# Mamba step sizes in later states, and the 64 sequences cut 11, 14, 14, 14, 11

## The chip, the cores and the metric

The kernel runs on one core of a Trainium2 chip. The core has five engines that run their own instruction queues in order and wait for one another on semaphores: TensorE (PE; its weight loads are PEld), VectorE (DVE), ScalarE (ACT), GpSimd (POOL) and SyncE (SP), which issues most transfers. The metric is device time in microseconds of a whole execution.

## The reference

The program is one audio tower of several layers; the change touches the first attention layer only. There a three-layer Mamba and a two-way LSTM run on the same input, and their outputs are fused. There are 64 sequences of S = 33 time steps. The part that is timed here is the Mamba step-size dt and the state scan:

```python
xdbl = jnp.einsum('blc,ec->ble', u, xpw)
dt = jax.nn.softplus(jnp.einsum('blr,cr->blc', dt_in, dw) + db)
A = -jnp.exp(Alog)
def step(h, inp):
    dt_t, B_t, C_t, u_t = inp
    dA = jnp.exp(dt_t[..., None] * A)
    h = dA * h + (dt_t * u_t)[..., None] * B_t[:, None, :]
    y = jnp.einsum('bcn,bn->bc', h, C_t)
...
y = ys.transpose(1, 0, 2) + u * Dp
y = y * _silu(z)
```

u is a causal convolution of the input's first projection (four taps), z the second half of the projection. There are 256 channels (two halves of 128, called h) and 16 states for each channel.

## The kernel before

The Mamba stage is `mamba_lstm`. The 64 sequences are cut into five **chunks** (`SEQS`, line 414), and each chunk of each of the three layers is an **item** j = 0 to 14; `item(j)` (line 430) gives layer, first column and number of columns n (sequences x 33). Within an item the loop runs over the 16 **states** k = 0 to 15; g = 16 j + k counts all 240. Channels lie on the partitions, and the two channel halves lie side by side, so that an operation over both is "double-width" (858 columns for 13 sequences).

One state takes one step of a four-engine pipeline:
- ScalarE, `decay(g)`, line 894: dA = exp(dt * A), two operations into a PSUM pair; it may run two states ahead of the scan (dA has two buffers).
- GpSimd, line 1126: dBu = du * B, also two states ahead.
- VectorE, `scan(g)`, line 1053, the recurrence over all sequences of the chunk (h restarts because dA is 0 at each first step), then `weigh(g - 1)`, line 1063: times C.
- TensorE, `add(g - 1)`: two matmuls with the identity (each runs as two passes) that sum the states in PSUM bank pair py.

SyncE loads B and C for two states at a time, four buffers deep.

Beside the states run, at fixed k, the preparation of later items and the end of earlier ones. All engines' order is written out by hand: in its loop over g each engine does its state work first and then whatever its own table of k says. What matters here, for item j:
- TensorE: the deltas (input of softplus) of item j+1 at k = 0 and 1; the convolution of item j+2 at k = 3 and 5 (`project`, one channel half each, eight passes), z at 7 and 8; LSTM matmuls at 2, 6 and 14.
- ScalarE: softplus of item j+1, in a form that is exact for large and small values and takes a chain of operations on `mag`, `e` and `low`: `delta` at k = 3, 4, 5 and `steps` at 7 and 8. u of item j+2 is copied out of PSUM at k = 7 and 8 (line 781), each copy waiting for one half of the convolution. Four small LSTM gate operations stand at k = 2, 6 and 10 (`lstm_gates`, lines 871 and 872, the last writes cz), the cell's tanh at 3, 7, 11 (line 876). Two table loads stand at k = 7 and 9 in the items with LSTM, two around the silu at k = 11.
- VectorE: the LSTM cell `lstm_c` at k = 1, 5 and 9 (line 1025 first; it needs the gates that ScalarE makes at k = 2, 6 and 10), `lstm_h` behind it at 2, 6, 10; the gate product yz of item j-1 at k = 1; at k = 8 `soften(j + 1)` (three double-width operations, lines 995, 998, 1003: dt, then du = dt * u) and `back(j - 2)` (line 1017, layer norm's scaling into m).
- GpSimd at k = 10 waits for du of item j+1 and for m.

The LSTM has 33 time steps, three to an item, and so fills items 0 to 10. In front of the loop everything for item 0 is prepared in one go (the head), and behind it the last item goes through output projection, layer norm and fusion (the tail).

Of the kernel before, what the change touches and what calls it, by code (L numbers as in the profile page):

```python
# [15 lines left out]
S = 33  # L16
# [393 lines left out]
    _at += _width  # L410
MWID = _at

SQ = 13
SEQS = [13, 13, 13, 13, 12]
NSC = len(SEQS)
SCW = SQ * S
NI = NL * NSC
LAST = NI - NSC
BG, NBS = 2, 4
# [10 lines left out]
def item(j):  # L430

    l, c = j // NSC, j % NSC
    return l, c * SCW, SEQS[c] * S


def by_seq(ap):
# [4 lines left out]
def mamba_lstm(nc, cst, w_dram, cw_dram, lstm_dram, xn, m, hT, norm):  # L441

    with ExitStack() as ctx:
# [313 lines left out]
        def _(act):  # L757
# [45 lines left out]
            def delta(j, k):  # L803
                l, at, n = item(j)
                if k == 3 or k == 4:
                    h = k - 3
                    act.wait_ge(d_ready, 2 * j + h + 1)
                    if j >= 1:
                        act.wait_ge(dt_done, j)
                    a(mag[:, h, 0:n], bank(j, f"d{h}")[:, 0:n], ACT.Abs).then_inc(mag_ready, 1)  # L810
                    a(pos[:, h, 0:n], bank(j, f"d{h}")[:, 0:n], ACT.Relu).then_inc(d_read, 1)
                if k == 4:
                    act.wait_ge(mag_ready, 2 * j + 2)
                    a(e[:, :, 0:n], mag[:, :, 0:n], ACT.Exp, scale=-1.0).then_inc(e_ready, 1)
                if k == 5:
                    a(low[:, :, 0:n], mag[:, :, 0:n], ACT.Relu, scale=-1.0, bias=edge[:, 4:5]).then_inc(capped, 1)
                    act.wait_ge(capped, j + 1)
                    a(low[:, :, 0:n], low[:, :, 0:n], ACT.Exp, scale=-1.0, bias=edge[:, 4:5]).then_inc(w_ready, 1)
                    act.wait_ge(w_ready, j + 1)
                    a(low[:, :, 0:n], low[:, :, 0:n], ACT.Square, scale=KAPPA, bias=edge[:, 1:2]).then_inc(sq_w_ready, 1)  # L820

            def steps(j, k):
                l, at, n = item(j)
                if k == 7:
                    act.wait_ge(sq_w_ready, j + 1)
                    a(low[:, :, 0:n], low[:, :, 0:n], ACT.Ln, bias=edge[:, 2:3]).then_inc(low_logged, 1)
                    act.wait_ge(e_ready, j + 1)
                    a(e[:, :, 0:n], e[:, :, 0:n], ACT.Ln, bias=edge[:, 0:1]).then_inc(ln_ready, 1)
                if k == 8:
                    act.wait_ge(low_logged, j + 1)  # L830
                    a(low[:, :, 0:n], low[:, :, 0:n], ACT.Exp, scale=-0.5, bias=edge[:, 3:4]).then_inc(low_ready, 1)

# [75 lines left out]
            project(0, 14)  # L908
            for k in (3, 4, 5):
                delta(0, k)  # L910
            for k in (7, 8):
                steps(0, k)
            act.wait_ge(l_loaded, 112)
            a(whh[:, :, :, :], whh[:, :, :, :], ACT.Copy, scale=0.5).then_inc(lw_ready, 1)
# [17 lines left out]
            for g in range(NI * DST):  # L932
# [18 lines left out]
                    project(j + 2, k)  # L951
                if k == 7 and j < LSTM_ITEMS:
                    nc.scalar.preload_act_table_set("natural_log_exp_and_others")
                if k in (7, 8) and j + 1 < NI:
                    steps(j + 1, k)
                if k == 7 and j >= 2:
                    logs(j - 2)
                if k == 9 and j < LSTM_ITEMS:
                    nc.scalar.preload_act_table_set("exp_and_others")
                if j == NI - 1 and k == 10:  # L960
# [22 lines left out]
        def _(dve):  # L983
# [83 lines left out]
            for g in range(NI * DST):  # L1067
                j, k = g // DST, g % DST
                scan(g)
                if g >= 1:  # L1070
                    weigh(g - 1)
                if j < LSTM_ITEMS:
                    if k in (1 if j else 2, 5, 9):
                        lstm_c(PER_ITEM * j + (k - 1) // 4)
                    if k in (2 if j else 3, 6, 10):
                        lstm_h(PER_ITEM * j + (k - 2) // 4)
                if j >= 1 and k == 1:
                    gate(j - 1)
                if k == 8:
                    if j + 1 < NI:  # L1080
                        soften(j + 1)
                    if j >= 2:
                        back(j - 2)
                if k == 15 and j >= LAST + 2:
                    fuse(j - LAST - 2)
            weigh(NI * DST - 1)
# [7 lines left out]
        def _(pool):  # L1094
# [16 lines left out]
            for g in range(NI * DST):  # L1111
                j, k = g // DST, g % DST
                l, at, n = item(j)
                q = g // BG
                if k == 0:
                    pool.wait_ge(du_done, j + 1)
                if k == 10:
                    if j + 1 < NI:
                        pool.wait_ge(du_done, j + 2)
                    if j >= 2:  # L1120
                        pool.wait_ge(m_scaled, j - 1)
                if g % BG == 0:
                    pool.wait_ge(b_loaded[q % NBS], 16 * (q // NBS + 1))
                if g >= 2:
                    pool.wait_ge(h_ready, g - 1)
                g_.tensor_tensor(dBu[:, g % 2, 0:2 * n].rearrange("p (a n) -> p a n", a=2), du[:, j % 2, :, 0:n],  # L1126
                                 Bs[:, q % NBS, k % BG, 0:n].unsqueeze(1).broadcast_to([128, 2, n]), ALU.mult).then_inc(dBu_ready, 1)
                if j in (1, NSC + 1) and k in (2, 4, 6, 8):
                    build(l + 1, k // 2 - 1)
# [2765 lines left out]
```

## Time and profile before

| | us |
|---|---|
| runs (3): median | 2210.42 |
| lowest and highest | 2202.44, 2212.16 |
| the profiled execution | 2202.75 |
| its span | 2200.9 |
| TensorE busy | 1873.3 (85%) |
| VectorE busy | 1626.5 (74%) |
| ScalarE busy | 1327.4 (60%) |
| GpSimd busy | 1013.3 (46%) |

The span is the time between first and last instruction. Shares are over the whole program; the Mamba stage is only its first 840 us or so, after which other layers with other limits follow. An engine's row in the timeline gives the start, the duration, what it does, and in brackets how long the engine sat idle before it and which operation of which engine ended that.

### The profile page before, as it was taken

How to read it: one execution, taken by the hardware profiler on the slowest of the kernel's cores; microseconds unless marked ns; L12 is line 12 of the kernel's file. 1: busy time of each engine (PE TensorE's matmuls, PEld its weight loads, DVE VectorE, ACT ScalarE, POOL GpSimd, SP SyncE). 2: the span in 40 equal slices, each digit the busy share in tenths (PEclk: the TensorE clock that was granted, in tenths of full speed). 3: DMA queues.
4: the chain of work that ended last, by engine and by line, in shares of the span. 5: the costliest groups of instructions: out<-in, count | busy, mean ns of one | idle time of the engine just before them, and what ended most of it. 6: DMA issues, size and time to landing. Idle time of an engine off the chain costs nothing. (4 is left out here: it accounts for less than half of the span.)

```text
span 2200.9 us, 49437 instructions
## 1 busy us (share of the span) xinstructions
PE 1873.3 (85%) x19547; PEld 1375.3 (62%) x19547; DVE 1626.5 (74%) x2594; ACT 1327.4 (60%) x2696; POOL 1013.3 (46%) x778
## 2 busy tenths in 40 slices
PE   7888888888888678987877777798688699999999
PEld 4444444444443335445667777767676599999999
DVE  3999999999999994867653332336544588998897
ACT  5777787778877643133533334252346488888886
POOL 1777777777777780100046666400350033333333
PEclk9999999999999998997889889899798699999999
DMA  3444444444444432600057777501640321121100
GB/s 128 160 133 130 124 147 134 129 129 127 138 137 141 140 111 54 136 8 7 21 178 214 214 217 219 151 10 41 222 145 15 145 88 52 66 74 61 33 6 7
DMA packets 98037, 241.63 MB, mean 110 GB/s; under 512 B 15024, under 2 KB 48320, under 8 KB 95504
## 3 DMA queue, kind: packets, MB, share of 16 engines
q1 hardware_dynamic: 89120, 218.12, 32.5%
q0 software_dynamic: 7680, 15.74, 2.8%
q10 hardware_dynamic: 1008, 4.62, 0.6%
q8 instruction: 155, 2.54, 0.5%
q14 instruction: 74, 0.61, 0.1%
HBM read 226.25 MB, written 12.19 MB: 108 GB/s over the span
## 5 line engine op out<-in xcount | busy, mean ns | idle before, releaser
L1126 POOL TENSOR_TENSOR dBu<-du,Bs 128x858 f32<-128x858 f32 (+1 forms) x240 | 589.7, 2459 | 198.2 <-DVE hst L1053 109.4
L576 PE MATMUL py<-hst,ident 128*128 128x429 f32 (+1 forms) x960 | 402.1, 546 | 82.2 <-DVE hst L1063 81.6
L1053 DVE TENSOR_TENSOR_SCAN hst<-dA,dBu 128x858 f32<-128x858 f32 (+1 forms) x240 | 457.7, 1907 | 12.3 <-ACT dA L894 9.2
L894 ACT ACTIVATE dA<-dt,negA 128x416 f32<-128x416 f32 (+1 forms) x480 | 269.6, 596 | 147.6 <-DVE hst L1053 146.7
L576 PEld LDWEIGHTS py<-hst,ident 128*128 128x128 f32 x960 | 178.5, 197 | 271.1 <-DVE hst L1063 153.1
L3451 POOL TENSOR_TENSOR hm<-h,mw 128x264 f32<-128x264 f32 x128 | 90.0, 703 | 390.6 <-DVE h L3431 390.6
L1063 DVE TENSOR_TENSOR hst<-hst,Cs 128x858 f32<-128x858 f32 (+1 forms) x240 | 247.1, 1030 | 0.0
L3322 PE MATMUL pg<-hs,wh 128*128 128x66 f16 x6144 | 218.0, 193 | 6.6 <-issue 6.3
L3322 PE MATMUL pg<-xm,wi 128*128 128x66 f16 x6144 | 216.1, 195 | 4.2 <-issue 2.9
L2848 ACT ACTIVATE eh<-ph,wb 128x128 f32<-128x128 f32 x384 | 108.9, 371 | 172.5 <-PE ph L2721 115.6
L3322 PEld LDWEIGHTS pg<-hs,wh 128*128 128x128 f16 x6144 | 203.9, 98 | 10.6 <-issue 7.2
L3322 PEld LDWEIGHTS pg<-xm,wi 128*128 128x128 f16 x6144 | 203.4, 98 | 8.6 <-issue 3.3
L2721 PE MATMUL ph<-xT,wb 128*128 128x128 f32 x768 | 120.0, 306 | 55.9 <-DVE xT L2780 49.4
L2786 DVE COPY yo<-po 128x128 f32<-128x128 f32 x96 | 27.7, 288 | 174.9 <-PE po L2731 100.1
L3372 ACT ACTIVATE pg<-bz 128x1188 f32<-128x1188 f32 x128 | 149.1, 1165 | 6.2 <-PE pg L3317 2.2
L2721 PEld LDWEIGHTS ph<-xT,wb 128*128 128x128 f32 x768 | 106.8, 215 | 65.0 <-DVE xT L2780 56.7
L2695 POOL DMA_INDIRECT expert_rows<-yo,give x96 | 94.9, 989 | 74.8 <-DVE yo L2786 56.3
L3421 DVE TENSOR_TENSOR prod<-z 128x528 f32<-128x528 f32 x128 | 111.6, 872 | 17.0 <-ACT z L3382 16.7
L2690 POOL DMA_INDIRECT xi<-token_rows,take x96 | 93.6, 975 | 44.8 <-issue 43.9
L2731 PE MATMUL po<-wb,eh 128*128 128x128 f32 x768 | 111.1, 292 | 0.0
L2731 PEld LDWEIGHTS po<-wb,eh 128*128 128x128 f32 x768 | 103.8, 210 | 0.1
L3381 ACT ACTIVATE z<-pg,scale 128x528 f32<-128x528 f32 x128 | 88.2, 689 | 24.0 <-PE pg L3322 22.9
(567 smaller groups left out, 3417.2 us busy)
## 6 DMA issues: line engine op xcount, KB each, us to landing
wb<-sf_w SPq DMA_DIRECT2D x96, 514.0 KB
Bs<-bc_rows SPq DMA_DIRECT2D x96, 429.0 KB, 4.6
Cs<-bc_rows SPq DMA_DIRECT2D x96, 429.0 KB, 3.5
mw<-route_weights SPq DMA_DIRECT2D x8, 2112.0 KB, 10.1
wb<-gf_w SPq DMA_DIRECT2D x24, 514.0 KB
Bs<-bc_rows SPq DMA_DIRECT2D x24, 396.0 KB, 5.2
Cs<-bc_rows SPq DMA_DIRECT2D x24, 396.0 KB, 4.6
mb<-route_masks SPq DMA_DIRECT2D x8, 1088.0 KB, 12.6
```

What stands on the lines that cost most here:

```text
L576: return nc.tensor.matmul(out, weight, moving, **kw)
L894: last = a(o, by_seq(dt[:, j % 2, h, 0:n])[:, :, 1:S], ACT.Exp, scale=negA[:, l, h * DST + k:h * DST + k + 1])
L1053: v.tensor_tensor_scan(hst[:, g % HR, 0:2 * n], dA[:, g % 2, 0:2 * n], dBu[:, g % 2, 0:2 * n], 0.0, ALU.mult, ALU.add).then_inc(h_ready, 1)
L1063: v.tensor_tensor(h, h, Cs[:, q % NBS, k % BG, 0:n].unsqueeze(1).broadcast_to([128, 2, n]), ALU.mult).then_inc(weighed, 1)
L1126: g_.tensor_tensor(dBu[:, g % 2, 0:2 * n].rearrange("p (a n) -> p a n", a=2), du[:, j % 2, :, 0:n], Bs[:, q % NBS, k % BG, 0:n].unsqueeze( ...
L2695: pool.indirect_dma_start(ys, bass.IndirectOffsetOnAxis(ap=give[:, d:d + 1], axis=0), yo[:, d % UN, :], None).then_inc(given[d % UN][0], 16)
L2721: last = nc.tensor.matmul(ph[:, j % 2, f * ST:(f + 1) * ST], wb[:, j % UN, f * 128:(f + 1) * 128], xT[:, j % UN, :], start=True, stop=True)
L2731: last = nc.tensor.matmul(po[:, j % 2, 0:D], eh[:, j % 3, f, :], wb[:, j % UN, F + f * D:F + (f + 1) * D], start=(f == 0), stop=(f == FC - 1))
L2848: last = nc.scalar.activation(eh[:, j % 3, f, :], ph[:, j % 2, f * ST:(f + 1) * ST], act_fn, bias=wb[:, j % UN, W1 + W2 + f:W1 + W2 + f + 1])
L3322: return nc.tensor.matmul(pg[q][:, bank, c:c + CB], (wh if u else wi)[:, wp, q * HE + e, GO[z_] * D:(GO[z_] + 1) * D], rhs, start=False, s ...
L3372: a(pg[q][:, :, 0:PERB * CB], bz[:, q, :, :], ACT.Copy).then_inc(seeded[q], 1)
L3421: link(v.tensor_tensor(prod[:, q, :, :], z[:, q, 0:2, :], z[:, q, 3:5, :], ALU.mult))
```

## The change

Two things.

The chunks become 11, 14, 14, 14 and 11 sequences instead of 13, 13, 13, 13 and 12. They are no longer of equal width, so first columns come from a table `SEQ0`, and the tiles are sized for 14 sequences.

ScalarE's chain for the next item's step sizes is spread over later states. Exp of -mag moves from k = 4 to 5 and stands beside the Relu into low; low's Exp and Square move from 5 to 8; the two logarithms from 7 to 9; the last Exp from 8 to 10. In the code `steps` now stands behind `logs`. VectorE's `soften` moves from k = 8 to 10, `back` stays at 8. GpSimd's wait for du moves from k = 10 to 12.

```diff
-SQ = 13
-SEQS = [13, 13, 13, 13, 12]
+SEQS = [11, 14, 14, 14, 11]
 NSC = len(SEQS)
-SCW = SQ * S
+SCW = max(SEQS) * S
+SEQ0 = [sum(SEQS[:c]) * S for c in range(NSC)]
...
-    return l, c * SCW, SEQS[c] * S
+    return l, SEQ0[c], SEQS[c] * S
...
-                if k == 4:
+                if k == 5:
                     act.wait_ge(mag_ready, 2 * j + 2)
                     a(e[:, :, 0:n], mag[:, :, 0:n], ACT.Exp, scale=-1.0).then_inc(e_ready, 1)
-                if k == 5:
                     a(low[:, :, 0:n], mag[:, :, 0:n], ACT.Relu, scale=-1.0, bias=edge[:, 4:5]).then_inc(capped, 1)
+
+            def steps(j, k):
+                l, at, n = item(j)
+                if k == 8:
                     act.wait_ge(capped, j + 1)
...
-            def steps(j, k):
-                l, at, n = item(j)
-                if k == 7:
+                if k == 9:
                     act.wait_ge(sq_w_ready, j + 1)
...
-                if k == 8:
+                if k == 10:
                     act.wait_ge(low_logged, j + 1)
...
-            for k in (7, 8):
+            for k in (8, 9, 10):
                 steps(0, k)
...
-                if k in (7, 8) and j + 1 < NI:
-                    steps(j + 1, k)
                 if k == 7 and j >= 2:
                     logs(j - 2)
+                if k in (8, 9, 10) and j + 1 < NI:
+                    steps(j + 1, k)
...
-                if k == 8:
-                    if j + 1 < NI:
-                        soften(j + 1)
-                    if j >= 2:
-                        back(j - 2)
+                if k == 8 and j >= 2:
+                    back(j - 2)
+                if k == 10 and j + 1 < NI:
+                    soften(j + 1)
...
-                if k == 10:
-                    if j + 1 < NI:
-                        pool.wait_ge(du_done, j + 2)
-                    if j >= 2:
-                        pool.wait_ge(m_scaled, j - 1)
+                if k == 10 and j >= 2:
+                    pool.wait_ge(m_scaled, j - 1)
+                if k == 12 and j + 1 < NI:
+                    pool.wait_ge(du_done, j + 2)
```

The order on ScalarE in item 5, from the decay of state 5 (first row) to the LSTM gates of state 6 (cz), before:

```order
L894 ACTIVATE dA<-dt,negA 128x13x32 x2
L816 ACTIVATE low<-mag,edge 128x858
L818 ACTIVATE low<-low,edge 128x858
L820 ACTIVATE low<-low,edge 128x858
L894 ACTIVATE dA<-dt,negA 128x13x32 x2
L871 ACTIVATE gate_ps<-gate_ps,lb 128x64 x3
L872 ACTIVATE cz<-gate_ps,lb 128x64
```

The same place in the changed kernel, where the item has 11 sequences and the next 14:

```order
L894 ACTIVATE dA<-dt,negA 128x11x32 x2
L814 ACTIVATE e<-mag 128x924
L815 ACTIVATE low<-mag,edge 128x924
L894 ACTIVATE dA<-dt,negA 128x11x32 x2
L871 ACTIVATE gate_ps<-gate_ps,lb 128x64 x3
L872 ACTIVATE cz<-gate_ps,lb 128x64
```

Three chain operations stood between the two decays, now there are two; one of the two came from in front of the first row.

ScalarE in item 5 from the decay of state 8 to the gates of state 10, before (the rows of `low` and `e` are the chain; 781 is the copy of u):

```order
L894 ACTIVATE dA<-dt,negA 128x13x32 x2
L854 ACTIVATE rstd<-rstd 128x429
L882 ACTIVATE hs<-hr 64x64 x2
L781 ACTIVATE u<-side,w 128x429
L831 ACTIVATE low<-low,edge 128x858
L894 ACTIVATE dA<-dt,negA 128x13x32 x2
L959 ACT_TABLE_LOAD
L894 ACTIVATE dA<-dt,negA 128x13x32 x2
L871 ACTIVATE gate_ps<-gate_ps,lb 128x64 x3
L872 ACTIVATE cz<-gate_ps,lb 128x64
```

And in the changed kernel:

```order
L894 ACTIVATE dA<-dt,negA 128x11x32 x2
L854 ACTIVATE rstd<-rstd 128x462
L882 ACTIVATE hs<-hr 64x64 x2
L781 ACTIVATE u<-side,w 128x462
L821 ACTIVATE low<-low,edge 128x924
L823 ACTIVATE low<-low,edge 128x924
L894 ACTIVATE dA<-dt,negA 128x11x32 x2
L826 ACTIVATE low<-low,edge 128x924
L828 ACTIVATE e<-e,edge 128x924
L959 ACT_TABLE_LOAD
L894 ACTIVATE dA<-dt,negA 128x11x32 x2
L871 ACTIVATE gate_ps<-gate_ps,lb 128x64 x3
```

One chain operation stood between these decays and the gates; now there are four.

VectorE in item 5 from the scan of state 8 to the LSTM cell of state 9, before:

```order
L1053 SCALAR_TENSOR_TENSOR hst<-dA,dBu 128x858
L1063 TENSOR_TENSOR hst<-hst,Cs 128x858
L995 TENSOR_TENSOR e<-pos,e 128x858
L998 TENSOR_TENSOR dt<-e,low 128x858
L1003 TENSOR_TENSOR du<-dt,u 128x858
L1017 SCALAR_TENSOR_TENSOR m<-cent,w,rstd 128x429
L1053 SCALAR_TENSOR_TENSOR hst<-dA,dBu 128x858
L1063 TENSOR_TENSOR hst<-hst,Cs 128x858
L1025 SCALAR_TENSOR_TENSOR ig<-gate_ps,cz 128x64
```

In the changed kernel, up to the softening:

```order
L1053 SCALAR_TENSOR_TENSOR hst<-dA,dBu 128x726
L1063 TENSOR_TENSOR hst<-hst,Cs 128x726
L1017 SCALAR_TENSOR_TENSOR m<-cent,w,rstd 128x462
L1053 SCALAR_TENSOR_TENSOR hst<-dA,dBu 128x726
L1063 TENSOR_TENSOR hst<-hst,Cs 128x726
L1025 SCALAR_TENSOR_TENSOR ig<-gate_ps,cz 128x64
L1027 SCALAR_TENSOR_TENSOR gate_ps<-gate_ps,cz 128x64
L1030 SCALAR_TENSOR_TENSOR cz<-gate_ps,ig 128x64
L1053 SCALAR_TENSOR_TENSOR hst<-dA,dBu 128x726
L1063 TENSOR_TENSOR hst<-hst,Cs 128x726
L1037 SCALAR_TENSOR_TENSOR hr<-gate_ps,tc 128x64
L995 TENSOR_TENSOR e<-pos,e 128x924
```

The three softening operations stood ahead of the cell's first row (1025) and now stand behind the cell and the scan of state 10.

## Rows read from the trace of the kernel before

**Rows 1.** Stretch: length; busy us (count) of PE, PEld, DVE, ACT, POOL; clock; DMA.

```profile
100.00:840.00 740.00, 626.36 (x2163) 319.29 (x2164) 711.17 (x644) 544.22 (x1023) 557.34 (x232) 0.97 0.44 130
```

**Rows 2.** Groups by form, 40 to 860 us: busy us, mean ns, idle before.

```profile
L1053 DVE TENSOR_TENSOR_SCAN hst<-dA,dBu 128x858 f32<-128x858 f32 x192 | 371.4, 1935 | 9.8 <-ACT dA L894 6.7 <-POOL dBu L1126 2.1 <-issue 0.2
L1063 DVE TENSOR_TENSOR hst<-hst,Cs 128x858 f32<-128x858 f32 x192 | 200.9, 1047 | 0.0
L1053 DVE TENSOR_TENSOR_SCAN hst<-dA,dBu 128x792 f32<-128x792 f32 x48 | 86.2, 1797 | 2.5 <-ACT dA L894 2.5
L1063 DVE TENSOR_TENSOR hst<-hst,Cs 128x792 f32<-128x792 f32 x48 | 46.2, 963 | 0.0
```

**Rows 3.** VectorE's waits, in total: first two 100 to 627 us, then 45 to 100.

```profile
DVE ig L1025 <- ACT cz L872: 13.1, 10, 1.9
DVE hst L1053 <- ACT dA L894: 5.4, 16, 0.6
...
DVE hst L1053 <- ACT dA L894: 3.5, 3, 2.6
...
DVE ig L1025 <- ACT cz L872: 1.9, 1, 1.9
```

**Rows 4.** VectorE's timeline, item 5, then item 6's yz: start us, us, operation.

```profile
322.99 0.97 DVE L1011 TENSOR_TENSOR yz<-sz,py 128x792 f32<-128x792 f32 x1
...
335.78 0.23 DVE L1025 SCALAR_TENSOR_TENSOR ig<-gate_ps,cz 128x64 f32<-128x64 f32 x1 [0.50 <-ACT cz L872]
...
342.39 1.95 DVE L1053 TENSOR_TENSOR_SCAN hst<-dA,dBu 128x858 f32<-128x858 f32 x1 [0.27 <-ACT dA L894]
...
345.20 1.05 DVE L995 TENSOR_TENSOR e<-pos,e 128x858 f32<-128x858 f32 x1
...
348.40 0.66 DVE L1017 SCALAR_TENSOR_TENSOR m<-cent,w,rstd 128x429 f32<-128x429 f32 x1
...
376.29 1.04 DVE L1011 TENSOR_TENSOR yz<-sz,py 128x858 f32<-128x858 f32 x1
```

**Rows 5.** Timeline of ScalarE in item 5.

```profile
333.78 1.12 ACT L894 ACTIVATE dA<-dt,negA 128x416 f32<-128x416 f32 x2
...
336.70 0.26 ACT L876 ACTIVATE tc<-cz 128x64 f32<-128x64 f32 x1
...
338.77 1.01 ACT L826 ACTIVATE low<-low,edge 128x858 f32<-128x858 f32 x1
...
340.59 0.64 ACT L838 ACTIVATE rstd<-var,eps 128x429 f32<-128x429 f32 x1
...
343.18 0.62 ACT L781 ACTIVATE u<-side,w 128x429 f32<-128x429 f32 x1
...
345.75 1.28 ACT L959 ACT_TABLE_LOAD   x1
...
348.71 0.32 ACT L872 ACTIVATE cz<-gate_ps,lb 128x64 f32<-128x64 f32 x1
```

**Rows 6.** Timeline of TensorE in items 5, 4 and 6 (x8: passes).

```profile
335.54 3.04 PE L576 MATMUL py<-hst,ident 128*128 128x429 f32 x8
338.42 2.91 PE L576 MATMUL side<-m,wt 128*128 128x429 f32 x8
...
284.19 2.82 PE L576 MATMUL py<-hst,ident 128*128 128x396 f32 x8
...
393.47 2.92 PE L576 MATMUL side<-m,wt 128*128 128x429 f32 x8
```

**Rows 7.** Stretches of the first 17 us of items 5 and 6, columns as above.

```profile
322.00:339.00 17.00, 15.34 (x61) 8.62 (x61) 16.43 (x19) 14.41 (x29) 13.08 (x6) 1.00 0.49 137
375.00:392.00 17.00, 14.90 (x55) 8.20 (x55) 15.63 (x18) 12.32 (x27) 14.21 (x7) 0.90 0.48 133
```

**Rows 8.** Timeline at item 0: the first scan, and the convolution of item 2.

```profile
48.94 3.78 DVE L1053 TENSOR_TENSOR_SCAN hst<-dA,dBu 128x858 f32<-128x858 f32 x2 [2.11 <-POOL dBu L1126]
...
73.46 2.91 PE L576 MATMUL side<-xn,wt 128*128 128x429 f32 x8
```

## The prediction

> **What bounds the kernel now.** I read the Mamba stage only, since the change touches nothing behind it. First the stretches: from 100 to 840 us VectorE is busy 711.17 of 740 us, so it is the bound, and only its idle time can be won [rows 1]. Then its costs by form: a state of a 13-sequence chunk takes a scan of 1935 ns and a weighting by C of 1047 ns, which overlap a little, so 2.80 us from scan to scan; one of a 12-sequence chunk takes 1797 and 963 ns [rows 2]. That is about 0.21 us for each sequence, with almost nothing fixed, and 64 sequences and 240 states stay 64 and 240: **cutting the chunks differently doesn't change VectorE's work**. Then who VectorE waits for. In items 1 to 10 (an item is one chunk in one layer) it waits for ScalarE's LSTM gates, once per item behind the fifth state, 13.1 us, and for ScalarE's decays dA, 5.4 us; together 18.5 us. Item 0 adds 3.5 and 1.9 us [rows 3]. The timeline of item 5 shows where: the wait of 0.50 us stands at state 5, that of 0.27 us at state 8 [rows 4]. In front of the first ScalarE ran the chain's three operations between the decays of states 5 and 6, in front of the second its two logarithms, the table load and more.
>
> **What the new order removes.** Two double-width operations (Exp and Square) leave the place between state 5's decay and the LSTM gates of state 6. Two such operations take 1.82 us where two logarithms stand together (338.77 to 340.59) [rows 5], so about 1.9 us with their dependence. No wait at state 5 was longer than 1.9 us: all ten go. State 7 loses its two logarithms, so the decay waits of state 8 go, and with softening at state 10 VectorE has 3.2 us of other work ahead of state 11, which covers those of state 12. **Removed: 18.5 us**, plus up to 1.9 us in item 0.
>
> **What it adds.** Softening (three VectorE operations, 345.20 to 348.40, 3.2 us [rows 4]) stood at state 8 and gave ScalarE that time before VectorE needed the gates at state 9, which ScalarE makes behind the decay of state 10. Now softening stands behind those gates, and four double-width operations of the chain stand before them. VectorE reaches the gates earlier and ScalarE later. I count both from the end of the gate product yz at 323.96 (322.99 + 0.97) in item 5.
> - VectorE without waits: to state 5's gates 11.3 us (335.78 - 0.50), from there to state 8's scan 6.35 (to 342.39 - 0.27), that state 2.8 (to 345.20), m 0.6, state 9 2.8: **23.85 us** [rows 4].
> - TensorE: the second half of the next-but-one item's convolution ends at 338.42 + 2.91 = 341.33, **17.4 us** after yz; TensorE runs without a gap up to there [rows 6]. ScalarE reads it in the u copy of state 8, which stands ahead of the moved Exp and Square.
> - ScalarE from there: u 0.5, Exp and Square 1.9, decay 9 1.1, two logarithms 1.9, then table load, decay 10 and gates 3.3 (345.75 to 349.03): **8.7 us** [rows 5].
>
> 17.4 + 8.7 - 23.85 = **2.2 us** of waiting at state 9 (partly at scan 9, for its decay), for chunks of 13. Today nothing shows there, since softening covers it.
>
> **A rule weighed.** From the small tanh at 336.70 to the logarithm at 338.77 lie 2.07 us, with the tanh, a u copy of 0.62 and a table load inside, so a load costs about 1.3 us [rows 5]. The Trainium skill, ScalarE: Activation LUTs, under What ACT_TABLE_LOAD costs, puts every switch at 1283 ns plus a drain of 1380 ns. One load now lies in the critical 8.7 us of eleven items; by the page these would be 1.4 us longer each and the sum 15 us more. The trace disagrees (2.07 us leave no room for it), so it has no part in the sum.
>
> **The chunk sizes.** Let n be this chunk, n' the next, n'' the one after. Eight TensorE passes over 429 columns take 3.04 us and over 396 2.82 us [rows 6]: 0.22 us per sequence. Up to the convolution's end 24 passes go with n (0.66 us per sequence) and 16 with n'' (0.4). VectorE's eight states go with n at 8 x 0.21 = 1.7, ScalarE's decays at under 0.1 each, its four chain operations with n' at 0.25. So the wait changes by **-0.9 per sequence of n, +0.25 of n', +0.4 of n''**: a small chunk gives VectorE less to do while its neighbours' preparation stays big. From 2.2 us:
> - items 1, 6 (14, 14, 14): 1.95
> - items 2, 7 (14, 14, 11): 0.75 by TensorE, 1.0 by ScalarE, which gets there later
> - items 3, 8 (14, 11, 11): 0 by the same step, 0.2 by ScalarE
> - items 4, 9 (11, 11, 14): 3.9
> - items 5, 10 (11, 14, 14): 4.65
>
> Twice each: **23.4 us**. Then the clock. In items 1, 2, 3, 6, 7 and 8 TensorE ran part of the first 17 us at 1.2 GHz (mean 0.90, against 1.00 in the four others) [rows 7], and the convolution ended 19.06 us after yz (item 6: 393.47 + 2.92, yz from 376.29 + 1.04) [rows 4, 6]: 1.7 us later. Before, state 5's wait took that up; now state 9's does. These are just the items that get 14 sequences. VectorE's scan, weighting and yz, which TensorE sits out before it begins an item, grow more with n than TensorE's own part, so I keep all six: 6 x 1.7 less the 0.8 that items 2, 3, 7 and 8 had to spare = **9.4 us**.
>
> Items 1 to 10: 23.4 + 9.4 - 18.5 = **+14.3 us**.
>
> Item 0 by the same steps, from its first scan at 48.94: the convolution of item 2 ends at 73.46 + 2.91, 27.4 us later [rows 8]; with 11, 14, 14 about 26.6, and 8.85 of ScalarE, against 10 states of 2.38 and 1.4 of LSTM work on VectorE, 25.2: 10.3 us of waits, now 5.4 (3.5 + 1.9) [rows 3]. **+4.9 us**.
>
> The head: the first scan waits for the whole preparation of item 0. With 11 instead of 13 sequences, 24 passes are 1.3 us shorter [rows 6], seven double-width ScalarE operations and their narrow ones 0.9, three VectorE operations 0.4, GpSimd's first product 0.3 (of the 2.11 us in which the scan waited for it) [rows 8]. **-2.9 us**. The tail goes from 12 to 11: some twelve passes and eight small operations, **-0.4 us**; the fusion of a 14-sequence chunk beside it eats some.
>
> Moved at no cost: GpSimd's wait for softening goes from state 10 to 12, behind softening by two states as before; its queue holds only the products, and its mean product of 2.40 us (557.34 over 232) against a step of 2.80 [rows 1, 2] says that it keeps up. SyncE's B and C transfers keep their places; they are released by products and weightings whose pace doesn't change. The items behind 10 have no LSTM gates, so nobody waits at state 9. If GpSimd's cover goes, that is a rival below.
>
> **Sum**: +14.3 + 4.9 - 2.9 - 0.4 = **+15.9 us**. The profiled execution took 2202.75 us (span 2200.9), 7.7 below the median of the runs, 2210.42; its sum is 2218.7. I add the difference to the median: **2226 us**. A measurement of this kernel can tell about 0.5%, 11 us, from no change.
>
> **The rivals.**
> 1. *The wait just goes* (faster). ScalarE gets to state 10's gates before VectorE, all waits behind the fifth state vanish: -18.5 - 1.9 - 3.3 = -24 us, 2187. It decides at 4.7 us in the 11-sequence items: ScalarE or TensorE would have to be that much earlier than item 5 shows. For it speaks that ScalarE is idle at times; against it, that this idle time lies at states 11 to 15 and 0 to 4. Chance 0.11.
> 2. *TensorE isn't late.* Then ScalarE's own work sets state 8: after the LSTM cell at 335.82, 2.07 us to the logarithm's place and 2.59 (340.59 to 343.18) to u, 16.6 us after yz instead of 17.4 [rows 4, 5]. Some 1 us less in six items, the slow clock hidden: about 0 in sum, 2210. Chance 0.20.
> 3. *The slow stretches go* because VectorE's waits lie elsewhere: 9.4 us less, +6.5, 2217. Chance 0.13.
> 4. *GpSimd falls behind in small chunks.* A product of 11 sequences must fit in 2.38 us; its mean is 2.40 now [rows 1], in proportion to the columns it would be 2.1, with no gain 2.4. If each of the 96 states of the six small items were 0.1 us over: +10 on top, 2236. Chance 0.07.
>
> My forecast has 0.49. **Range 2205 to 2240**: it takes in cases 2 to 4 and the spread of the runs, and leaves out the first. Slower by over 0.5%: 0.49 + 0.07 = 0.56; within: 0.33; faster: 0.11.
>
> **What would show it.** VectorE's waits for the gates: none at state 5, but 2 to 6 us at state 9 (scan 9 and ig together), biggest in items 0, 5, 10, 4 and 9; their sum in items 1 to 10 about 33 us. The u copy of state 8 released by TensorE. Decay waits at states 8 and 12 gone. The first scan near 46 us. VectorE's busy time the same within 3 us. Wrong: waits at state 9 under 1 us in the small items (case 1), a GpSimd release in front of the scans (case 4), a granted clock of 1.00 in the 14-sequence items (case 3).

## The result, and the profile after

| | before | after |
|---|---|---|
| median of six runs, us | 2203.19 | 2226.00 |
| lowest and highest | 2202.44, 2212.16 | 2220.92, 2233.27 |
| the profiled execution | 2202.75 | 2226.15 |
| its span | 2200.9 | 2224.3 |

The change makes the kernel slower: ratio 1.0095, 95% interval 1.0076 to 1.0114. The forecast was 2226 us, and that is the measured median. Part of this agreement is luck: the forecast added 15.9 us to 2210.42, the median of three runs, and with three more runs the median of the kernel before is 2203.19, so the measured difference is 22.8 us. One of its terms was also wrong, and another wait of nearly the same size, which the forecast didn't have, stood in for it, as the waits below show.

I measure the Mamba stage by its last instruction, VectorE's last fusion (line 1043). It ended at 844.23 us before and ends at 864.97 now (864.38 + 0.59), **20.7 us later**. The rest of the program isn't touched by the change; it holds the other 2.7 us of the 23.4 by which the two profiled executions differ. From the timeline of VectorE: the first scan (to be read beside the one of before in [rows 8]), and the stage's last row.

```profile
45.84 3.23 DVE L1053 TENSOR_TENSOR_SCAN hst<-dA,dBu 128x726 f32<-128x726 f32 x2 [1.71 <-POOL dBu L1124]
...
864.38 0.59 DVE L1043 SCALAR_TENSOR_TENSOR hT<-py,fb,hT 128x363 f32<-128x363 f32 x1 [1.60 <-PE py L576]
```

The first scan comes at 45.84 instead of 48.94: -3.1 us, where -2.9 was forecast. VectorE's work is the same. First the page's two groups over all scans and weightings (busy, mean ns, idle before), then the same by form from 40 to 880 us:

```profile
L1053 DVE TENSOR_TENSOR_SCAN hst<-dA,dBu 128x924 f32<-128x924 f32 (+1 forms) x240 | 457.2, 1905 | 17.7 <-ACT dA L894 11.7
L1063 DVE TENSOR_TENSOR hst<-hst,Cs 128x924 f32<-128x924 f32 (+1 forms) x240 | 246.7, 1028 | 0.0
```

```profile
L1053 DVE TENSOR_TENSOR_SCAN hst<-dA,dBu 128x924 f32<-128x924 f32 x144 | 298.0, 2070 | 0.7 <-ACT dA L894 0.4 <-issue 0.2
...
L1053 DVE TENSOR_TENSOR_SCAN hst<-dA,dBu 128x726 f32<-128x726 f32 x96 | 159.1, 1659 | 17.0 <-ACT dA L894 11.2 <-POOL dBu L1124 5.2 <-PE py L576 0.6
```

The scans took 371.4 + 86.2 = 457.6 us before [rows 2] and take 457.2 now. What is new is idle time, and nearly all of what precedes a scan stands in the 11-sequence chunks (17.0 us against 0.7). VectorE's waits in items 1 to 10, 97 to 640 us (waiting operation, releaser: us in total, times, longest):

```profile
DVE ig L1025 <- ACT cz L872: 26.9, 17, 3.1
DVE hst L1053 <- ACT dA L894: 4.9, 3, 2.2
DVE hst L1053 <- POOL dBu L1124: 3.5, 2, 1.7
DVE hst L1053 <- PE py L576: 0.6, 1, 0.6
```

That is 35.9 us, and 0.2 without a cause (its third row names the wrong engine, as shown further down), against 18.5 before [rows 3] (19.0 with 0.5 of small waits for TensorE and without a cause). By the state at which they stand, from the timeline, us:

| where | before | forecast | measured |
|---|---|---|---|
| state 5, and decays of 8 and 12 | 18.5 | 0 | 0 |
| state 9 (gates, decay, product) | 0 | 23.4 | 23.8 |
| slow clock at the item's start | (in state 5) | 9.4 | 0 |
| state 1, gates | 0 | 0 | 10.9 |
| small ones | 0.5 | | 1.3 |

State 9, item by item, forecast (without the clock's term) and measured:

| items | forecast | measured |
|---|---|---|
| 1, 6 | 1.95 | 2.96, 1.04 |
| 2, 7 | 1.0 | 0.95, 0.63 |
| 3, 8 | 0.2 | 0.36, 0.37 |
| 4, 9 | 3.9 | 3.97, 3.96 |
| 5, 10 | 4.65 | 4.78, 4.80 |

Item 5 shows the mechanism. From the timeline of the engines, in order of time:

```profile
343.52 3.12 PE L576 MATMUL side<-m,wt 128*128 128x462 f32 x8
...
346.69 0.65 ACT L781 ACTIVATE u<-side,w 128x462 f32<-128x462 f32 x1 [0.84 <-PE side L576]
347.23 1.06 ACT L821 ACTIVATE low<-low,edge 128x924 f32<-128x924 f32 x1
348.32 1.07 ACT L823 ACTIVATE low<-low,edge 128x924 f32<-128x924 f32 x1
...
350.44 1.67 DVE L1053 TENSOR_TENSOR_SCAN hst<-dA,dBu 128x726 f32<-128x726 f32 x1 [2.21 <-ACT dA L894]
...
352.28 1.28 ACT L959 ACT_TABLE_LOAD   x1
...
355.13 0.32 ACT L872 ACTIVATE cz<-gate_ps,lb 128x64 f32<-128x64 f32 x1
...
355.48 0.22 DVE L1025 SCALAR_TENSOR_TENSOR ig<-gate_ps,cz 128x64 f32<-128x64 f32 x1 [2.57 <-ACT cz L872]
```

The convolution ends at 346.64 (343.52 + 3.12) and releases the copy of u; ScalarE has the last gate at 355.45 (355.13 + 0.32), 8.8 us behind the convolution's end, where the forecast had 8.7. VectorE, with nothing to do, waits twice for it, 2.21 and 2.57 us. Before, the softening at 345.20 [rows 4] filled this place.

### The profile page after: what moved, and what is told of

It reads as the page before. It is cut to its first block and busy times, and to the rows that moved or that the text cites. A ratio compares the mean times of both kernels' runs of the same rounds, so it can differ in the third digit from the quotient of the medians.

```text
span 2224.3 us, 49425 instructions
## 1 busy us (share of the span) xinstructions
PE 1881.6 (85%) x19547; PEld 1377.8 (62%) x19547; DVE 1627.7 (73%) x2594; ACT 1325.2 (60%) x2696; POOL 1005.5 (45%) x778
## 5 line engine op out<-in xcount | busy, mean ns | idle before, releaser
L1124 POOL TENSOR_TENSOR dBu<-du,Bs 128x924 f32<-128x924 f32 (+1 forms) x240 | 582.0, 2426 | 228.4 <-DVE hst L1053 105.0
L576 PE MATMUL py<-hst,ident 128*128 128x462 f32 (+1 forms) x960 | 411.7, 560 | 80.5 <-DVE hst L1063 80.4
L1053 DVE TENSOR_TENSOR_SCAN hst<-dA,dBu 128x924 f32<-128x924 f32 (+1 forms) x240 | 457.2, 1905 | 17.7 <-ACT dA L894 11.7
L576 PEld LDWEIGHTS py<-hst,ident 128*128 128x128 f32 x960 | 186.1, 202 | 264.0 <-DVE hst L1063 120.3
L894 ACT ACTIVATE dA<-dt,negA 128x448 f32<-128x448 f32 (+1 forms) x480 | 270.4, 598 | 116.5 <-DVE hst L1053 115.2
L1063 DVE TENSOR_TENSOR hst<-hst,Cs 128x924 f32<-128x924 f32 (+1 forms) x240 | 246.7, 1028 | 0.0
L3320 PEld LDWEIGHTS pg<-xm,wi 128*128 128x128 f16 x6144 | 202.5, 98 | 10.6 <-issue 5.2
```

The source lines that it names most:

```text
L576: return nc.tensor.matmul(out, weight, moving, **kw)
L894: last = a(o, by_seq(dt[:, j % 2, h, 0:n])[:, :, 1:S], ACT.Exp, scale=negA[:, l, h * DST + k:h * DST + k + 1])
L1053: v.tensor_tensor_scan(hst[:, g % HR, 0:2 * n], dA[:, g % 2, 0:2 * n], dBu[:, g % 2, 0:2 * n], 0.0, ALU.mult, ALU.add).then_inc(h_ready, 1)
L1063: v.tensor_tensor(h, h, Cs[:, q % NBS, k % BG, 0:n].unsqueeze(1).broadcast_to([128, 2, n]), ALU.mult).then_inc(weighed, 1)
L3320: return nc.tensor.matmul(pg[q][:, bank, c:c + CB], (wh if u else wi)[:, wp, q * HE + e, GO[z_] * D:(GO[z_] + 1) * D], rhs, start=False, s ...
```

## Experiments

"Stage end" is the end of the Mamba stage in the run's own trace, as above (844.23 before, 864.97 after); "waits" are VectorE's waits in items 1 to 10 in that trace (19.0 before, 36.1 after). The ratio is that of the whole program to the kernel before on the same chip. Its medians there were 2154.36 us (the first four runs), 2153.79 (the next four) and 2205.07 (the last two). The stage can be compared across them only roughly: the first scan of the chunks of 13 starts within 48.7 and 49.2 us in all, that of the chunks of 11 within 45.3 and 46.3, and the stage of two almost equal kernels (runs 4 and 10), on the chips at 2154 and at 2205, ends within 2.1 us (838.17 and 836.07) though their spans are 48 us apart. The ratio carries the scatter of all that follows the stage, the stage end that of one execution, so differences of 2 us or less between two stages are not shown by these runs. The waits of item 0 are counted behind its first scan; what the first scan itself waits for belongs to the head.

### 1 and 2. Each half of the change alone

The changed kernel with the old sizes:

```diff
-SEQS = [11, 14, 14, 14, 11]
+SEQS = [13, 13, 13, 13, 12]
```

> The later chain alone, with the chunks of before (13, 13, 13, 13, 12). Theory: softening no longer covers ScalarE at state 9, whatever the chunk size, and only the size of the wait depends on the chunk. Waits for ScalarE at state 9 of about 2.3 us in each of items 1 to 10 (23 us), waits at state 5 gone, head unchanged (first scan near 48.9 us), some 3 to 10 us more at state 1 from TensorE's slow stretches. Against before: +8 to +16 us, ratio 1.004 to 1.007. Rival (the loss is the chunk cut, the order is harmless): waits at state 9 under 1 us, ratio 0.993 to 1.001.

The kernel before with the new sizes:

```diff
-SEQS = [13, 13, 13, 13, 12]
+SEQS = [11, 14, 14, 14, 11]
...
-    return l, c * SCW, SEQS[c] * S
+    return l, SEQ0[c], SEQS[c] * S
```

> The chunks 11, 14, 14, 14, 11 alone, with the order of before. Theory: softening at state 8 still covers state 9; the small chunks lengthen the waits that stand at state 5 and at the decays of states 8 and 12 (about 1.6 and 1.9 us in an 11-sequence item), the 14-sequence ones shorten them; head 3 us shorter. Ratio 0.999 to 1.003, and together with the order alone less than the 21 us that both cost: the remainder, some 5 to 10 us, is their product. Rival (the cut is the loss): ratio 1.006 to 1.009.

| | ratio | stage end | item 0, waits | items 1 to 10, waits |
|---|---|---|---|---|
| order alone | 1.0109 [1.0055, 1.0162] | 862.41 (+18.2) | 9.8 | 30.1 |
| sizes alone | 1.0024 [1.0003, 1.0045] | 844.82 (+0.6) | 7.5 | 20.9 |
| both | 1.0095 [1.0076, 1.0114] | 864.97 (+20.7) | 10.5 | 36.1 |

VectorE's waits with the order alone, 97 to 640 us:

```profile
DVE ig L1025 <- ACT cz L872: 25.6, 15, 3.2
DVE hst L1053 <- ACT dA L894: 4.3, 6, 1.7
```

and with the sizes alone:

```profile
DVE ig L1025 <- ACT cz L872: 11.5, 9, 1.9
DVE hst L1053 <- ACT dA L894: 8.8, 9, 1.1
```

The order costs nearly all of it. With chunks of 13 items 5 and 10 wait 2.32 us at state 9, each, where the prediction's step gave 2.2; the ten items together wait 24.9 us there and 4.9 at state 1. With the order alone items 1 to 10 wait 11.1 us more than before, item 0 4.4, and two fusions behind item 10 wait 4.2 for TensorE; that makes 19.7, and 1.5 us less were lost, for which these waits don't account. The loss and the ratio lie above what I expected (8 to 16 us, 1.004 to 1.007), which had only items 1 to 10. The sizes alone cost next to nothing in the stage: the first scan comes 3.6 us earlier (45.32), item 0 waits 2.1 us more and items 1 to 10 2.0 more; the whole program comes out slower by 0.24%, with an interval just above 1. Together the two make 1.9 us more than their sum, where I expected 5 to 10, and the whole program doesn't show even that (1.0095 for both, 1.0109 for the order alone). The sizes move the waits of state 9 from the large chunks into the small ones (0.4 to 4.8 us, instead of 1.0 to 3.7), and leave their sum as it was, 24.9 and 23.8.

### 3. ScalarE's copy of z ahead of the logarithms

In the changed kernel TensorE waits 22.2 us for ScalarE's raw copy of z (line 786), which stands behind the late gates; before it waited 10.6 us there. TensorE's waits in the changed kernel, same stretch:

```profile
PE py L576 <- DVE hst L1063: 42.9, 15, 4.8
PE side L576 <- ACT sz L786: 22.2, 10, 3.1
```

This run puts the copy one state earlier, ahead of the logarithms, table load and gates:

```diff
-                if k == 10:
+                if k == 9:
                     if j >= 3:
                         act.wait_ge(y_gated, j - 2)
```

> The changed kernel with one move: ScalarE's copy of raw z out of the shared PSUM bank stands at state 9, in front of the two logarithms, and not behind the gates of state 10. Theory: the waits at state 1 (10.9 us in items 2 to 10 of the changed kernel) come from TensorE, which sits out that copy and softening, falls to a lower granted clock and finishes its backlog late; with the copy early TensorE's wait for it (22.2 us in ten items) falls under 8 us and the waits at state 1 to under 5 us, while state 9 grows by the copy, 0.5 us an item. Net against the changed kernel: 0 to -6 us. Rival (state 1 waits for ScalarE's own backlog): state 1 unchanged, net +4 us.

Measured: ratio 1.0252 [1.0199, 1.0304], stage end 889.80, 24.8 us later than the changed kernel. I had expected 0 to 6 us less, and the rival said 4 us more; both missed this by far. TensorE's wait for the copy is gone, but the copy now stands in ScalarE's queue before z is made. From its waits, and from its timeline in item 5:

```profile
ACT sz L786 <- PE side L576: 19.6, 9, 2.3
```

```profile
366.03 0.56 ACT L786 ACTIVATE sz<-side 128x462 f32<-128x462 f32 x1 [1.81 <-PE side L576]
```

The chain's logarithms, the table load and the gates stand behind it. VectorE waited 4.89 us for the gates there instead of 2.57, and the waits at state 9 are 51.6 us instead of 23.8. So each microsecond in front of ScalarE's gates is VectorE's: 1.81 of waiting and 0.56 of copy are 2.37, and VectorE's wait grew by 2.32. The waits at state 1 went from 10.9 to 8.2 only, so the run doesn't tell how much of them the copy of z makes.

### 4 and 5. Softening as cover, in front of the LSTM cell and behind it

The first of these two keeps most of the new order with chunks of 13, but starts `steps` a state earlier (Exp and Square at k = 7, logarithms at 8, last Exp at 9), copies u's second half at 9, and softens at k = 9 *in front of* the LSTM cell. In ScalarE's loop `steps` stands ahead of `logs` again, and GpSimd waits for du at k = 11; these edits, and the new state of u's copy, are left out of the cut below.

```diff
-                if k == 8:
+                if k == 7:
                     act.wait_ge(capped, j + 1)
...
-                if k == 9:
+                if k == 8:
                     act.wait_ge(sq_w_ready, j + 1)
...
-                if k == 10:
+                if k == 9:
                     act.wait_ge(low_logged, j + 1)
...
+                if k == 9 and j + 1 < NI:
+                    soften(j + 1)
                 if j < LSTM_ITEMS:
                     if k in (1 if j else 2, 5, 9):
...
-                if k == 10 and j + 1 < NI:
-                    soften(j + 1)
```

> Chunks 13, 13, 13, 13, 12, softening at state 9 in front of the LSTM cell, the chain at states 5, 7, 8 and 9 (Relu; Exp and Square behind the table load; two logarithms; last Exp), and ScalarE's u copy of state 8 behind the decay of state 9. Theory (softening must stand between the chain and the gates that VectorE needs next, as cover): no wait at state 9's cell, decay waits of 0.4 to 1 us at state 9, none at states 5 and 8; 18 us of waits become 4 to 9. Ratio 0.994 to 0.997. Rival (any spreading costs as much as it gives, since ScalarE is full from state 4 to 11): ratio 1.000 to 1.005.

The second differs from it in VectorE's softening, which stands at k = 10 again, behind the cell, and with it in GpSimd's wait, at 12 (not in the cut).

```diff
-                if k == 9 and j + 1 < NI:
-                    soften(j + 1)
...
+                if k == 10 and j + 1 < NI:
+                    soften(j + 1)
```

> e4_soften_at_9 with one move: VectorE softens at state 10, behind the LSTM cell of state 9, and not in front of it (GpSimd's wait at 12 again). ScalarE's order is that of e4. Theory (softening is the cover of the gates): the waits for the gates at state 9 come back, about 2 us in each of items 1 to 10 (e4 has none there), and the Mamba stage ends some 15 to 25 us later than in e4; ratio to before 1.002 to 1.008. Rival (what helped in e4 was ScalarE's order, above all the earlier Exp and Square): ratio 0.995 to 0.999, waits at state 9 under 0.5 us.

| | ratio | stage end | waits |
|---|---|---|---|
| softening in front of the cell | 0.9957 [0.9933, 0.9981] | 838.17 (-6.1) | 12.5 |
| softening behind the cell | 1.0079 [1.0053, 1.0105] | 858.85 (+14.6) | 30.9 |

VectorE's waits, in front of the cell:

```profile
DVE hst L1053 <- ACT dA L894: 11.7, 21, 1.5
DVE ig L1025 <- ACT cz L872: 0.5, 1, 0.5
```

and behind it:

```profile
DVE ig L1025 <- ACT cz L872: 23.9, 17, 2.9
DVE hst L1053 <- ACT dA L894: 6.7, 13, 1.5
```

Both runs came as expected, and the rival (that ScalarE's order is what helps) fell: ScalarE's order is the same in both. The place of three VectorE operations, with GpSimd's wait behind them, is worth 20.7 us of the stage, and it is the waits for the gates that come and go with them (0.5 and 23.9). Item 5 with the softening in front:

```profile
344.81 1.05 DVE L995 TENSOR_TENSOR e<-pos,e 128x858 f32<-128x858 f32 x1
...
346.29 0.32 ACT L872 ACTIVATE cz<-gate_ps,lb 128x64 f32<-128x64 f32 x1
...
348.02 0.22 DVE L1025 SCALAR_TENSOR_TENSOR ig<-gate_ps,cz 128x64 f32<-128x64 f32 x1
```

ScalarE has the gates at 346.61. Without the softening VectorE would ask for them at 344.8. With it, it asks at 348.0. In the whole program this kernel beats the kernel before by 0.4%, the most of any run here; run 7 below, which differs in the cut alone, is the only other one whose interval lies below 1.

### 6. The gates ahead of the variance copy

The waits at state 1 stand behind ScalarE's copy of the variance (line 851), which waits for TensorE. From the timeline at the end of item 4 and the start of item 5 of the changed kernel, in order of time:

```profile
304.11 1.04 PE L576 MATMUL side<-m,w 128*128 128x462 f32 x2 [2.03 <-ACT sz L786]
...
312.07 2.71 PE L576 MATMUL py<-hst,ident 128*128 128x363 f32 x4 [2.78 <-DVE hst L1063]
...
326.31 0.94 PE L576 MATMUL side<-sq,avg 128*128 128x462 f32 x2
...
327.29 0.56 ACT L851 ACTIVATE var<-side 128x462 f32<-128x462 f32 x1 [3.08 <-PE side L576]
...
328.70 0.23 DVE L1025 SCALAR_TENSOR_TENSOR ig<-gate_ps,cz 128x64 f32<-128x64 f32 x1 [2.37 <-ACT cz L872]
```

The run puts the gates of k = 2 ahead of that copy, everything else as in the changed kernel:

```diff
+                if k in (2, 6, 10) and g != 2 and j < LSTM_ITEMS:
+                    lstm_gates(t + (k - 2) // 4)
                 if j >= 2 and k in (0, 2, 8, 12):
                     back(j - 2, k)
-                if j < LSTM_ITEMS:
-                    if k in (2, 6, 10) and g != 2:
-                        lstm_gates(t + (k - 2) // 4)
+                if j < LSTM_ITEMS:
```

> The changed kernel with one move: at state 2 ScalarE makes the LSTM gates before it copies the variance out of PSUM. Theory (TensorE is late at an item's end and ScalarE stands in the variance copy, with the gates that VectorE needs queued behind it): the waits at state 1 in items 2 to 10, 10.9 us in the changed kernel, fall under 3 us; state 9 unchanged at 24 us; the stage 6 to 10 us shorter than in the changed kernel, ratio to before 1.003 to 1.007. Rival (the gates themselves wait for TensorE's LSTM matmuls): waits at state 1 unchanged.

Measured: ratio 1.0098 [1.0067, 1.013], stage end 861.77 (3.2 us earlier than the changed kernel), waits 32.0. The waits at state 1 for the gates fell from 10.9 to 0.4 us. Half of them came back in another place, those at state 9 rose from 23.8 to 25.4, and item 0 waits 12.2 us instead of 10.5:

```profile
DVE ig L1025 <- ACT cz L872: 16.5, 11, 3.2
DVE hst L1053 <- ACT dA L894: 6.2, 4, 2.2
DVE yz L1011 <- PE py L576: 4.9, 5, 1.7
```

yz, right behind the cell, now waits for TensorE to add up the previous item. I had expected 6 to 10 us, under 3 us of waits at state 1 and a ratio of 1.003 to 1.007; 5.3 us of waits are left there, and the ratio isn't better than that of the changed kernel. So the queue order on ScalarE is one cause of the state-1 waits and TensorE's lateness at an item's end is the other.

### 7 and 8. Other cuts with the better order

Both are the kernel of run 4 with other sizes.

```diff
-SEQS = [13, 13, 13, 13, 12]
+SEQS = [12, 13, 13, 13, 13]
```

> e4_soften_at_9 with chunks 12, 13, 13, 13, 13 (the small one first). Theory (the head goes with the first chunk at about 1.5 us per sequence, VectorE's work doesn't change): first scan near 47.3 us, tail 0.3 us longer, 1 to 2 us less than e4; ratio 0.994 to 0.997. Rival (a small chunk in items 0, 5 and 10 costs what the head gives): equal to e4 or up to 2 us more.

```diff
-SEQS = [13, 13, 13, 13, 12]
+SEQS = [11, 14, 14, 14, 11]
```

> e4_soften_at_9 with the chunks 11, 14, 14, 14, 11. Theory (the cut is nearly neutral by itself: head 3.6 us shorter, longer waits in the small chunks, none in the large ones): Mamba stage within 5 us of e4, ratio 0.994 to 0.999. Rival (with the later order the small chunks do cost more): 5 to 12 us more than e4, ratio 0.999 to 1.002.

| | ratio | first scan | stage end | item 0 | items 1 to 10 |
|---|---|---|---|---|---|
| 13, 13, 13, 13, 12 (run 4) | 0.9957 [0.9933, 0.9981] | 48.75 | 838.17 | 6.4 | 12.5 |
| 12, 13, 13, 13, 13 | 0.9983 [0.9968, 0.9997] | 47.88 | 836.94 | 5.0 | 13.3 |
| 11, 14, 14, 14, 11 | 0.9996 [0.9977, 1.0015] | 46.22 | 843.26 | 9.5 | 17.7 |

A first chunk of 12 starts the scans 0.9 us earlier (1.5 expected), and its stage ends 1.2 us earlier, too little to be told from scatter; the ratio, 0.9983, lies just outside what I expected (0.994 to 0.997) and isn't better than that of run 4. The cut of the change costs 5.1 us with this order, at the lower end of what the rival said (5 to 12 us, ratio 0.999 to 1.002): 2.5 us of the head are won, 3.1 lost in item 0 and 5.2 in items 1 to 10, and behind item 10 0.8 come back. Nearly all its waits are for decays (16.2 of 17.7 us), and 13.5 us of the 17.7 stand in items 4, 5, 9 and 10, which have 11 sequences; I take it that a chunk of 11 gives ScalarE less time per state while it prepares one of 14:

```profile
DVE hst L1053 <- ACT dA L894: 16.2, 19, 1.9
```

### 9. Only Exp and Square moved, softening left

The smallest edit that takes away what I blamed for the waits at state 5: in the kernel before, low's Exp and Square go from k = 5 to 7, in front of the logarithms.

```diff
-                    act.wait_ge(capped, j + 1)
-                    a(low[:, :, 0:n], low[:, :, 0:n], ACT.Exp, scale=-1.0, bias=edge[:, 4:5]).then_inc(w_ready, 1)
-                    act.wait_ge(w_ready, j + 1)
-                    a(low[:, :, 0:n], low[:, :, 0:n], ACT.Square, scale=KAPPA, bias=edge[:, 1:2]).then_inc(sq_w_ready, 1)
...
                 if k == 7:
+                    act.wait_ge(capped, j + 1)
+                    a(low[:, :, 0:n], low[:, :, 0:n], ACT.Exp, scale=-1.0, bias=edge[:, 4:5]).then_inc(w_ready, 1)
+                    act.wait_ge(w_ready, j + 1)
+                    a(low[:, :, 0:n], low[:, :, 0:n], ACT.Square, scale=KAPPA, bias=edge[:, 1:2]).then_inc(sq_w_ready, 1)
```

> The kernel before with one move: low's Exp and Square go from state 5 to state 7, behind the table load; softening stays at state 8, chunks stay 13, 13, 13, 13, 12. It shows whether the waits at state 5 (13.1 us) can be won without moving softening. Theory (ScalarE is full from state 4 to 8, so the work only goes where the next wait is): waits at state 5 gone, the decay of state 8 late by about 2.5 us in each item instead of 0.2 to 0.6; items 1 to 10 wait 20 to 30 us; ratio 1.000 to 1.005. Rival (state 5 is the only tight place): decay waits at state 8 under 1 us, ratio 0.994 to 0.998.

Measured: ratio 1.0061 [1.0035, 1.0087], stage end 855.17 (+10.9), waits 26.6. This is what I expected, but for the ratio, which lies just above the range. The waits for gates at state 5 are gone altogether, which confirms the first term. In their place the scan of state 8 waits 23.1 us (2.2 before), 19.2 of them put down to ScalarE's decay. VectorE's waits for decays at all states:

```profile
DVE hst L1053 <- ACT dA L894: 22.4, 17, 3.2
```

ScalarE in item 5, in front of that decay:

```profile
342.73 1.28 ACT L953 ACT_TABLE_LOAD   x1
...
347.94 0.64 ACT L838 ACTIVATE rstd<-var,eps 128x429 f32<-128x429 f32 x1
348.48 1.13 ACT L894 ACTIVATE dA<-dt,negA 128x416 f32<-128x416 f32 x2
```

The table load, four chain operations (left out above, 344.03 to 347.94) and rstd take 5.75 us in front of the decay, and the scan pays 2.10 us of it. ScalarE is idle for a quarter of the stage [rows 1], but not here.

### 10. The better order with the gates first

Runs 4 and 6 together, chunks of 13: the order of run 4, and the gates ahead of the variance copy as in run 6 (the same diff).

> e4_soften_at_9 with ScalarE's gates in front of its variance copy at state 2. Theory: in e4 TensorE isn't late at the item's end, only 0.5 us of waits stand at state 1, so nothing is left to win there: Mamba stage within 1.5 us of e4, ratio 0.994 to 0.998. Rival (the variance copy holds the gates in every kernel): 3 us or more shorter than e4.

Measured: ratio 0.9988 [0.9969, 1.0008], stage end 836.07 (2.1 us earlier than run 4, on another chip; 1.5 at most and a ratio up to 0.998 were expected), waits 12.5, item 0 4.9 instead of 6.4. The sum of waits in items 1 to 10 is that of run 4, so nothing is shown to be won. The stage is as good as the best here; the whole program isn't told apart from the kernel before, nor from run 4, whose interval it overlaps. The 8.2 us that the stage won in the profiled executions are within what the layers behind it scatter (medians 2203.13 and 2205.07, single runs from 2195.44 to 2217.81).

## Why the prediction was right, point by point

**VectorE is the bound, and its work doesn't depend on the cut**: right. 457.2 and 246.7 us for scans and weightings, against 457.6 and 247.1.

**Removed 18.5 us**: right. In items 1 to 10 no wait at state 5, nor for the decays of 8 and 12, is left. Run 9 shows that it was the moved pair, Exp and Square, that caused those at state 5.

**Added 23.4 us at state 9**: right in mechanism and size, 23.8 measured, within 0.4 us in eight of ten items, and 1.0 off in items 1 and 6, up and down. Runs 4 and 5 show the mechanism: the softening is what hid ScalarE's lateness. Run 1 gives 2.3 us for items 5 and 10 at 13 sequences, forecast 2.2. In the other items of run 1 the wait was between 1.0 and 3.7. Part of the spread is the step's own: items 4 and 9, with 12 sequences, wait 3.2, and 2.2 + 0.9 is 3.1. Part is not: items 1 and 6 differ in nothing that the step knows and wait 3.72 and 1.03, so its agreement to 0.4 us by item is partly luck. In items 4 and 9 the trace puts 1.7 of the 4.0 us down to GpSimd's product, which would be a piece of rival 4. The timeline of item 4 says otherwise:

```profile
297.27 1.60 POOL L1124 TENSOR_TENSOR dBu<-du,Bs 128x726 f32<-128x726 f32 x1 [1.62 <-DVE m L1017]
...
297.78 1.02 ACT L894 ACTIVATE dA<-dt,negA 128x352 f32<-128x352 f32 x2
...
298.93 1.67 DVE L1053 TENSOR_TENSOR_SCAN hst<-dA,dBu 128x726 f32<-128x726 f32 x1 [1.73 <-POOL dBu L1124]
```

The product that m releases is that of state 10 (GpSimd's wait for m stands there), while the scan at 298.93 is that of state 9, whose product GpSimd had made before it began to wait, at 295.65. The product of state 10 merely ends at 298.87, right before the scan. What the scan needs is the decay of state 9, which ends at 298.80, behind the moved Exp and Square. So this too is ScalarE, as the step had it, and rival 4 didn't come: in items 1 to 10 no wait is left that can be laid at GpSimd (item 9 repeats the pattern).

**9.4 us for a slow clock at the start of the items with 14**: wrong, and this is the step that failed. I carried the mean granted clock of 0.90 of items 1, 2, 3, 6, 7 and 8 (item 6 in [rows 7]) over to the new order. In the changed kernel the same stretches, 17 us from about 2 us behind the item's first scan, run at 1.00 in all ten items. Item 6 (columns as in [rows 1]), beside that of before in [rows 7]:

```profile
377.00:394.00 17.00, 16.14 (x71) 9.24 (x68) 16.34 (x15) 11.98 (x28) 14.36 (x7) 1.00 0.44 135
```

That was rival 3, to which I gave 0.13. Ahead of these stretches TensorE waits for yz: 16.9 us in the ten items before, 10.5 in the changed kernel, where it comes later. But that wait alone doesn't set the clock. Item 6 of the kernel before, and the same place in run 9, whose chunks are the same:

```profile
377.38 2.96 PE L576 MATMUL py<-u,diag 128*128 128x429 f32 x4 [2.10 <-DVE yz L1011]
```

```profile
384.73 1.71 PE L576 MATMUL py<-u,diag 128*128 128x429 f32 x4 [2.10 <-DVE yz L1011]
```

The same wait of 2.10 us, and the four passes behind it take 2.96 us in one kernel (granted clock 0.50 from 378 to 380 us) and 1.71 in the other. The 1.7 us were thus no property of the place, and why these stretches ran at 1.00 stays open.

In the changed kernel the clock falls in another place, behind state 9, where TensorE waits first for the copy of z and then through the softening: between the scans of states 10 and 15 it is 0.67 to 0.91 in all ten items, and was 1.00 in nine of them before (0.76 in item 10). Item 4, about that stretch, and the same one before:

```profile
300.00:322.00 22.00, 17.18 (x40) 8.07 (x39) 19.59 (x22) 18.30 (x35) 13.56 (x7) 0.84 0.35 91
```

```profile
296.00:318.00 22.00, 16.65 (x62) 7.89 (x62) 21.36 (x21) 16.64 (x33) 17.39 (x8) 1.00 0.46 139
```

**In its place, 10.9 us at state 1**, which no step of the forecast held. TensorE comes late to the item's end, in item 4 after waits of 2.03 and 2.78 us and with four passes that take 2.71 us where they later take 1.39. ScalarE stands at its variance copy for it. From ScalarE's waits:

```profile
ACT var L851 <- PE side L576: 21.0, 9, 3.7
```

It was 2.9 us in nine waits before. Behind the copy in the queue stand the gates, and VectorE waits for those. Run 6 shows both parts. What isn't settled is how much of TensorE's lateness is the waiting itself and how much the clock that falls behind it: no run here separates the two.

**The rivals**: TensorE was late, as forecast, in six of the ten items: the copy of u at state 8 waits for it in items 1, 4, 5, 6, 9 and 10 (0.33 to 1.39 us, 5.1 in sum). In items 2, 3, 7 and 8 it doesn't wait; there ScalarE sets the time by itself, which is the way of rival 2 and also what the table of sizes had for these four (1.0 and 0.2 "by ScalarE"). The row of ScalarE's waits has ten, but four of them (2.6 us) are of the first half's copy, one state earlier:

```profile
ACT u L781 <- PE side L576: 7.7, 10, 1.4
```

Rival 1 fell with the first row of state 9.

**Item 0 +4.9**: right, +5.1 (10.5 from 5.4). **Head -2.9**: right, -3.1. **Tail -0.4**: wrong, though small. Behind item 10 the sum is +1.6, of which 1.8 are two waits of VectorE at the fusion of a chunk (line 1043) for TensorE, 1.36 us in item 12 and 0.40 in item 13.

The sum for the stage: -3.1 + 5.1 + 17.1 + 1.6 = +20.7, where I had -2.9 + 4.9 + 14.3 - 0.4 = +15.9. Of the 4.8 us between them 1.5 are the waits at state 1 beyond the wrong term of 9.4, 0.4 state 9, 0.9 small waits, and 2.0 the tail. That 10.9 us stood where I had 9.4 is chance: without the waits at state 1 the stage would have lost 9.8 us, near the 6.5 of rival 3, and not 15.9.

**Cost of the sizes**: with the new order alone the stage loses 18.2 us, with both 20.7, so the small chunks, which bear the longest waits in my table, are not what makes the change slow. The table tells where the waits stand, run 1 how much they are without the sizes.

## What to carry to other kernels

A long operation in front of a cross-engine wait is cover for the other engine's queue, even if nobody put it there for that: before moving it, add up what the other engine has between its last input from elsewhere and what is waited for. Moving work out from in front of one wait in a full queue moves the wait to the next reader (13.1 us at state 5 became 23.1 at state 8 in run 9); look for a place where the reader has other work, not for one where the queue's average is low. And a copy placed early to free another engine costs its wait to all that stands behind it (run 3).

## What the runs showed that I had not expected

TensorE's slow stretches moved with the waits: when VectorE's idle time went from state 5 to state 9, they left the starts of the items (0.90 to 1.00 in six of ten) and came up behind state 9 (0.84 over the 22 us of item 4). In item 4 the granted clock was 0.50 from 306 to 308 us, behind the wait of 2.03 us, and 0.52 behind that of 2.78, where four passes over 363 columns took 2.71 us instead of 1.39, about twice, which is the step between 2.4 and 1.2 GHz. Even the same wait at the same place doesn't always bring one (2.96 and 1.71 us above). A slow stretch measured at one place of a schedule is thus no cost of that place once the schedule changes.
